# The causal mask in two attention layers: added by VectorE in a buffer instead of by products on TensorE

## The chip, the cores and the metric

The kernel runs as one program on one core of a Trainium2 chip. The metric is the device time of one execution in microseconds (us); the median of several runs is compared. Five engines work side by side, each in its own order, and wait for one another by semaphores: PE (TensorE, the matrix engine), DVE (VectorE), ACT (ScalarE), POOL (GpSimd) and SP (SyncE, which only issues DMAs here). PE writes its products into PSUM; DVE and ACT read them there.

## The reference, cut to what matters

The model is a tower of nine layers over 32 utterances of T = 93 frames and 256 channels: a tokenizer, then attention and feed-forward layers in turn. Four of the layers are attentions, and all four run through the same helper functions. The two that are changed are the first (called gated, names that begin with `gattn`) and the second (routed, `rattn`); both have 16 heads of width 16 and a causal mask. The first one, for example:

```python
scores = jnp.einsum('bhqd,bhkd->bhqk', q, k) * scale
causal = jnp.tril(jnp.ones((s, s), dtype=bool))
scores = jnp.where(causal[None, None], scores, -jnp.inf)
probs = jax.nn.softmax(scores / TEMP, axis=-1)
probs = probs * gate
out = jnp.einsum('bhqk,bhkd->bhqd', probs, v)
```

The third (differential, `dattn`) has 32 causal maps for each utterance, the fourth (`eattn`) has 16 heads and no mask.

## The kernel before, in words

**What a map goes through.** Each utterance has 16 score maps of 93x93. Four maps make a unit (93x372 numbers, one PSUM bank); an utterance has four units, `w` = 0 to 3, in two pairs, `p` = 0 and 1. The scores are computed twice. The first time, with queries on the partitions (tile `scores`), they serve only to find the maximum of each row: DVE reduces each unit to `negmax`. The second time, turned (tile `scoresT`), the negated maxima are added by products with `maxT`, and ACT takes the exponential into `probs`. PE then weighs the values (`outputs`), DVE divides by the sums (`rden`, `ctx`), PE turns the result (`turn_ctx`, L581) and projects it (L593), and DVE adds it to `hidden`.

**Where the mask stands.** In a causal attention the mask of -1e30 has to be in the first scores before the maximum is taken. `scores(b, buf, p)` does it on PE: for each of the two units of a pair one product of the identity with `mask_q`, 372 columns in bf16 (L524), opens the bank, and the eight score products of the pair (L530) are added on top. In the turned scores the mask comes with `maxT` and is not touched by the change.

**The order on PE** is written out by hand in `utterance` of `attention_pe`. While utterance b is weighed, the first scores of b+1 are made: scores of pair 0 of b+1, turned scores of pair 0 of b, scores of pair 1 of b+1, `turn_ctx` of b-1, turned scores of pair 1, weighing of units 0 and 1, projection of b-1, weighing of units 2 and 3, `turn_max` (L540). Two utterances make one turn of a hardware loop. PE takes its instructions strictly in this order.

**The order on DVE** (`attention_dve`): the maxima of pair 0 (L663, twice), the division of b-1 (`context`: a reciprocal, L908, and a product, L909), the maxima of pair 1, the split of the maxima into two bf16 numbers (L671, L673), the addition of the output (L919, L921), the copy of `maxT` (L680) and a statistic of the new rows (L303).

**The waits around the change.** `scores` waits for the semaphore `maxed`, which each reduction raises, so the bank of the unit two before is free. `turn_ctx` waits for `ctx_ready`, which DVE raises after `context`. `cut` on POOL prepares the queries of the next utterance (L489) as soon as the turned scores of a pair are done.

Of the kernel before, what the change touches and what calls it, by code (L numbers as in the profile page):

```python
# [24 lines left out]
ALU = mybir.AluOpType  # L25
AX = mybir.AxisListType

P = 128
# [3 lines left out]
T = 93  # L32
# [4 lines left out]
GT = GU * T  # L37
# [314 lines left out]
class Attention:  # L352
# [11 lines left out]
    def __init__(self, s, maps, causal, exp_scale):  # L364
# [9 lines left out]
        self.k = s.sb("k", [P, 2, DC, T])  # L374
        self.only = s.sb("only", [P, self.variants])
        self.parts = maps // HEADS
        self.sel = s.sb("sel", [P, HEADS, T], BF16)
        self.negmax = s.sb("negmax", [P, maps])

# [5 lines left out]
        self.ctxT = s.sb("ctxT", [P, DC, T])  # L385
        if causal:
            self.mask_q = s.sb("mask_q", [P, 4, T], BF16)
        self.ps_s = s.ps("scores", [P, 2, 512])
        self.ps_t = s.ps("scoresT", [P, 2, 512])
        self.ps_o = s.ps("outputs", [P, 2, 512])  # L390
# [10 lines left out]
        self.cut_ready = s.sem("cut_ready")  # L401
        self.scored = s.sem("scored")
        self.maxed = s.sem("maxed")
        self.split_ready = s.sem("split_ready")
        self.max_turned = s.sem("max_turned")
        self.maxT_ready = s.sem("maxT_ready")
# [57 lines left out]
def attention_constants_dve(dve, a, ident):  # L464

    rows = ident[:, :].rearrange("p (h v e) -> p v h e", h=2, v=a.variants)
    dve.tensor_reduce(a.only[:, :], rows, AX.XY, ALU.add).then_inc(a.step, 1)
    dve.sem_inc(a.maxed, 2)
    dve.sem_inc(a.probs_ready, 2)
    dve.sem_inc(a.weighed, 4)  # L470
    dve.sem_inc(a.scoredT, 2 * a.units)
    dve.sem_inc(a.outputs_read, 3 - a.banks_o)
# [42 lines left out]
def attention_pe(pe, a, ident, ident16, w_out, before_out=None, extra_out=None):  # L515


    def scores(b, buf, p):
        if 2 * p % (a.units // DC) == 0:
            pe.wait_ge(a.cut_ready, DC * b + (2 * p * DC // a.units + 1))  # L520
        pe.wait_ge(a.maxed, b * a.units + (2 * p + 2))
        if a.causal:
            for half in range(2):
                pe.matmul(a.ps_s[0:T, half, 0:GT], ident16[:, 0:T], a.mask_q[:, :, :], start=True, stop=False,  # L524
                          skip_group_check=True)
        for j in range(4):
            for half in range(2):
                c, _, v = a.place(2 * p + half)
                rows = slice(half * P // 2, (half + 1) * P // 2)
                mm = pe.matmul(a.ps_s[0:T, half, j * T:(j + 1) * T], a.q[rows, buf, c, v + j, :], a.k[rows, buf, c, :],  # L530
                               start=not a.causal, stop=True, skip_group_check=True)
                if j == 3:
                    mm.then_inc(a.scored, 1)

# [83 lines left out]
    for p in range(a.units // 2):  # L618
        scores(0, 0, p)
# [36 lines left out]
def attention_dve(dve, a, steps, contexts, add, finish=None, shared=None):  # L656
# [1 line left out]

    def maximum(b, w):
        dve.wait_ge(a.scored, b * a.units + (w + 1))
        dve.tensor_reduce(a.negmax[0:T, a.first_map(w):a.first_map(w) + 4],  # L663
                          a.ps_s[0:T, w % 2, 0:GT].rearrange("p (j t) -> p j t", j=4), AX.X, ALU.max,
                          negate=True).then_inc(a.maxed, 1)

    def split(b):
        dve.wait_ge(a.maxed, 2 + (b + 1) * a.units)
# [26 lines left out]
    def utterance(b, buf, first, last):  # L695
        for p in range(a.units // 2):
            if not last:
                maximum(b + 1, 2 * p)
                maximum(b + 1, 2 * p + 1)
            if not first:  # L700
                behind(b - 1, 1 - buf, p)
        if not last:
            split(b + 1)
        if not first:
            add(b - 1)
        if not last:
            max_t(b + 1)
        if not first and shared is not None:
            measure_dve(dve, shared, b - 1, a.added, b)

    for w in range(a.units):
        maximum(0, w)
    split(0)
    max_t(0)
    over_utterances(dve, utterance)
# [2032 lines left out]
```

## Time and profile before

| what | us |
|---|---|
| median of 3 runs | 4184.95 |
| lowest and highest run | 4178.12, 4190.71 |
| the profiled execution, its own time | 4172.62 |
| its span, first to last instruction | 4170.9 |
| PE busy (79% of the span) | 3284.4 |
| DVE busy (50%) | 2086.2 |

A row of the trace names a line of the kernel (L524), an engine, an operation and the tiles out<-in. Matrix instructions overlap in their pipeline, so the distance from one start to the next tells more than their durations. The clock that TensorE was granted is shown as a share of full speed: 1.00 is 2.4 GHz and 0.50 is 1.2 GHz.

### The profile page before, as it was taken

How to read it: one execution, taken by the hardware profiler on the slowest of the kernel's cores; microseconds unless marked ns; L12 is line 12 of the kernel's file. 1: busy time of each engine (PE TensorE's matmuls, PEld its weight loads, DVE VectorE, ACT ScalarE, POOL GpSimd, SP SyncE). 2: the span in 40 equal slices, each digit the busy share in tenths (PEclk: the TensorE clock that was granted, in tenths of full speed). 3: DMA queues.
4: the chain of work that ended last, by engine and by line, in shares of the span. 5: the costliest groups of instructions: out<-in, count | busy, mean ns of one | idle time of the engine just before them, and what ended most of it. 6: DMA issues, size and time to landing. Idle time of an engine off the chain costs nothing. (4 is left out here: it accounts for less than half of the span.)

```text
span 4170.9 us, 70241 instructions
## 1 busy us (share of the span) xinstructions
PE 3284.4 (79%) x23447; PEld 2210.8 (53%) x23448; DVE 2086.2 (50%) x4029; ACT 1232.1 (30%) x2459; POOL 1221.4 (29%) x934
## 2 busy tenths in 40 slices
PE   7589981649997699999606996478888887579999
PEld 3357761326775367777505995234334333256777
DVE  0444437323445245555542333478888888731443
ACT  2222110011121122222213442265555565413222
POOL 0102110102120124334171002656556555510221
PEclk9698875778888899999658998689888888769998
DMA  1000000570000200000241112222212221100000
GB/s 46 12 1 0 0 2 11 88 97 1 0 0 11 88 1 0 0 0 0 70 137 50 45 50 60 74 58 54 52 46 58 52 52 52 36 10 0 9 11 10
DMA packets 250482, 140.02 MB, mean 34 GB/s; under 512 B 175329, under 2 KB 226467, under 8 KB 250384
## 3 DMA queue, kind: packets, MB, share of 16 engines
q1 hardware_dynamic: 230480, 122.61, 12.0%
q0 software_dynamic: 18432, 12.40, 1.3%
q10 hardware_dynamic: 1472, 3.85, 0.3%
q8 instruction: 43, 0.70, 0.1%
q14 instruction: 55, 0.45, 0.0%
HBM read 103.41 MB, written 35.21 MB: 33 GB/s over the span
## 5 line engine op out<-in xcount | busy, mean ns | idle before, releaser
L2414 DVE TENSOR_TENSOR_SCAN ssm_state<-ssm_dA,ssm_dBx 128x372 f32<-128x372 f32 x512 | 434.3, 910 | 103.3 <-ACT ssm_dA L2203 82.6
L2109 POOL TENSOR_TENSOR ssm_dBx<-ssm_du,ssm_bc_wide 128x1488 f32<-128x1488 f32 x128 | 426.9, 3340 | 196.5 <-DVE ssm_state L2414 195.1
L2288 PE MATMUL ssm_y<-ssm_hC,top_ident 128*128 128x512 f32 (+1 forms) x768 | 405.9, 671 | 93.8 <-DVE ssm_hC L2419 86.6
L2203 ACT ACTIVATE ssm_dA<-ssm_delta,ssm_decay 128x368 f32<-128x368 f32 x512 | 276.7, 565 | 190.9 <-DVE ssm_state L2414 179.2
L2288 PEld LDWEIGHTS ssm_y<-ssm_hC,top_ident 128*128 128x128 f32 x768 | 157.6, 216 | 307.9 <-issue 165.2
L2419 DVE TENSOR_TENSOR ssm_hC<-ssm_state,ssm_c_wide 128x1488 f32<-128x1488 f32 x128 | 218.1, 1704 | 5.1
L643 ACT ACTIVATE dattn_probs<-dattn_scoresT 93x372 f32<-93x372 f32 x256 | 108.1, 472 | 350.9 <-PE dattn_scoresT L556 350.9
L570 PE MATMUL dattn_outputs<-dattn_v,dattn_probs 93*93 (+1 forms) x2048 | 185.4, 233 | 0.0
L570 PEld LDWEIGHTS dattn_outputs<-dattn_v,dattn_probs 93*93 93x93 f32 x2048 | 181.8, 163 | 3.4
L489 POOL TENSOR_TENSOR rattn_q<-rattn_q_all,rattn_only 128x372 f32<-128x372 f32 x64 | 51.7, 807 | 439.6 <-PE rattn_scoresT L556 247.2
L1409 POOL TENSOR_TENSOR dattn_square<-dattn_square,top_minus_half 93x16 f32<-93x16 f32 x32 | 92.7, 2896 | 271.9 <-DVEq L1485 271.9
L489 POOL TENSOR_TENSOR eattn_q<-eattn_q_all,eattn_only 128x372 f32<-128x372 f32 x64 | 51.6, 807 | 403.3 <-PE eattn_scoresT L556 217.0
L663 DVE TENSOR_REDUCE dattn_negmax<-dattn_scores 93x4 f32<-93x372 f32 x256 | 127.1, 536 | 82.5 <-PE dattn_scores L530 79.7
L2251 PE MATMUL ssm_misc<-ssm_xT,ssm_w_tap 128*128 128x364 f32 (+3 forms) x512 | 165.9, 477 | 2.6 <-ACT ssm_conv L2140 2.0
L489 POOL TENSOR_TENSOR gattn_q<-gattn_q_all,gattn_only 128x372 f32<-128x372 f32 x64 | 51.7, 807 | 334.0 <-PE gattn_scoresT L556 248.8
L489 POOL TENSOR_TENSOR dattn_q<-dattn_q_all,dattn_only 128x744 f32<-128x744 f32 x64 | 91.6, 1432 | 170.6 <-ACT dattn_k_all L781 98.0
L1535 PE MATMUL tiles_hidden<-tiles_x_part,moe_w 128*128 128x256 bf16 x496 | 136.4, 275 | 3.0 <-DVE tiles_x_part L1889 3.0
L1901 DVE TENSOR_TENSOR tiles_act<-tiles_gelu,tiles_act 128x512 bf16<-128x512 f32 x124 | 85.8, 692 | 102.4 <-ACT tiles_act L1827 102.4
L1537 PE MATMUL tiles_hidden<-tiles_x_part,moe_w 128*128 128x256 bf16 x496 | 136.4, 275 | 0.0
L1536 PE MATMUL tiles_hidden<-tiles_x_part,moe_w 128*128 128x256 bf16 x496 | 136.4, 275 | 0.0
L2251 PEld LDWEIGHTS ssm_misc<-ssm_xT,ssm_w_tap 128*128 128x128 f32 x512 | 98.1, 192 | 70.5 <-issue 13.7
L1535 PE MATMUL tiles_product<-moe_w,tiles_act 128*128 x496 | 135.2, 273 | 0.0
(546 smaller groups left out, 7209.1 us busy)
## 6 DMA issues: line engine op xcount, KB each, us to landing
ssm_bc_wide<-bc_rows SPq DMA_DIRECT2D x128, 372.0 KB, 4.3
route_stage<-in_L_ffn_W SPq DMA_DIRECT2D x32, 512.0 KB, 4.2
qkv_rows<-rattn_rows SPq DMA_DIRECT2D x32, 288.0 KB, 3.1
rattn_heads<-qkv_rows SPq DMA_DIRECT2D x96, 96.0 KB, 3.5
moe_sent<-top_blank SPq DMA_DIRECT2D x1, 7936.0 KB, 23.6
tiles_x_in<-moe_sent SPq DMA_DIRECT2D x31, 256.0 KB, 2.8
moe_back<-tiles_y SPq DMA_DIRECT2D x31, 256.0 KB, 2.1
tok_frames<-in_frames ACTq DMA_DIRECT2D x8, 376.0 KB, 8.4
```

What stands on the lines that cost most here:

```text
L489: pool.tensor_tensor(a.q[:, buf, c, :, :], a.q_all[:, c, bass.ds(b * T, T)].unsqueeze(1).broadcast_to([P, a.variants, T]), a.only[:, :].un ...
L570: mm = pe.matmul(a.ps_o[0:T, bank, h * (HD + 1):(h + 1) * (HD + 1)], a.probs[0:T, w % 4, j * T:(j + 1) * T], a.v[0:T, b, h, :], start=True ...
L663: dve.tensor_reduce(a.negmax[0:T, a.first_map(w):a.first_map(w) + 4], a.ps_s[0:T, w % 2, 0:GT].rearrange("p (j t) -> p j t", j=4), AX.X, A ...
L1535: pe.matmul(out, w_high, x_high, start=start, stop=False)
L1536: pe.matmul(out, w_high, x_low, start=False, stop=False)
L1537: return pe.matmul(out, w_low, x_high, start=False, stop=stop)
L2109: pool.tensor_tensor(dBx[:, k % 2, :, :], du[:, :, :], bc_wide[:, q % BUFS, 0, k % 2, :].unsqueeze(1).broadcast_to([P, CC, GT]), ALU.mult) ...
L2203: act.activation(by_utterance(dA[:, ring(k, c), 0:GT])[:, :, 1:], by_utterance(delta[:, c, :])[:, :, 1:], ACT.Exp, scale=decay[:, c, k:k + ...
L2251: mm = pe.matmul(by_utterance(ps_m[:, 0:GT])[:, :, back:], w_tap[:, TAPS - 1 - back, c, m * P:(m + 1) * P], by_utterance(n.xT[:, c, :])[:, ...
L2288: mm = pe.matmul(ps_y[:, at], ident[:, :], hC[:, k % 2, :, :].rearrange("p c t -> p (c t)")[:, at], start=(k == 0), stop=(k == N - 1), ski ...
L2414: dve.tensor_tensor_scan(state[:, k % 2, c, :], dA[:, ring(k, c), 0:GT], dBx[:, k % 2, c, :], 0.0, ALU.mult, ALU.add).then_inc(scanned, 1)
L2419: dve.tensor_tensor(hC[:, k % 2, :, :], state[:, k % 2, :, :], ps_c[:, 0:GT].unsqueeze(1).broadcast_to([P, CC, GT]), ALU.mult).then_inc(hc ...
```

## The change

In attentions that are causal and have 16 maps (`masked_early`: gated and routed), `scores` loses its two mask products a pair, and the score products open their bank themselves. DVE adds `mask_q` to the scores of each unit and writes the sum as f32 into a new buffer `masked` in SBUF, and reduces the maxima from there. PE's wait for a free bank is on the new semaphore `scores_masked`, raised by the addition, in place of `maxed`. The differential attention keeps its products and the expert attention has no mask, but for these too the two reductions of a pair now stand behind both waits for the two units' scores.

```diff
@@ Attention.__init__
+        self.masked_early = causal and self.parts == 1
+            self.masked = s.sb("masked", [P, 2, 4, T]) if self.parts == 1 else None
+        self.scores_masked = s.sem("scores_masked")
@@ attention_constants_dve
+    dve.sem_inc(a.scores_masked, 2)
@@ attention_pe, scores
-        pe.wait_ge(a.maxed, b * a.units + (2 * p + 2))
-        if a.causal:
+        pe.wait_ge(a.scores_masked if a.masked_early else a.maxed, b * a.units + (2 * p + 2))
+        if a.causal and not a.masked_early:
             for half in range(2):
                 pe.matmul(a.ps_s[0:T, half, 0:GT], ident16[:, 0:T], a.mask_q[:, :, :], start=True, stop=False,
                           skip_group_check=True)
...
-                               start=not a.causal, stop=True, skip_group_check=True)
+                               start=not a.causal or a.masked_early, stop=True, skip_group_check=True)
@@ attention_dve
-    def maximum(b, w):
-        dve.wait_ge(a.scored, b * a.units + (w + 1))
-        dve.tensor_reduce(a.negmax[0:T, a.first_map(w):a.first_map(w) + 4],
-                          a.ps_s[0:T, w % 2, 0:GT].rearrange("p (j t) -> p j t", j=4), AX.X, ALU.max,
-                          negate=True).then_inc(a.maxed, 1)
+    def maxima(b, p):
+        for w in (2 * p, 2 * p + 1):
+            dve.wait_ge(a.scored, b * a.units + (w + 1))
+            if a.masked_early:
+                dve.wait_ge(a.maxed, b * a.units + (w + 1))
+                dve.tensor_tensor(a.masked[0:T, w % 2, :, :], a.ps_s[0:T, w % 2, 0:GT].rearrange("p (j t) -> p j t", j=4),
+                                  a.mask_q[0:T, :, :], ALU.add).then_inc(a.scores_masked, 1)
+        for w in (2 * p, 2 * p + 1):
+            if a.masked_early:
+                dve.wait_ge(a.scores_masked, b * a.units + (w + 3))
+                found = a.masked[0:T, w % 2, :, :]
+            else:
+                found = a.ps_s[0:T, w % 2, 0:GT].rearrange("p (j t) -> p j t", j=4)
+            dve.tensor_reduce(a.negmax[0:T, a.first_map(w):a.first_map(w) + 4], found, AX.X, ALU.max,
+                              negate=True).then_inc(a.maxed, 1)
```

How the instructions stand on PE at the head of the gated attention's loop, before (ISA and REGISTER_ALU are waits and counts of the sequencer; x8 means eight in a row):

```order
L521 ISA
L524 MATMUL gattn_scores<-gattn_mask_q,top_ident 93x372 x2
L530 MATMUL gattn_scores<-gattn_k,gattn_q 93x93 x8
L545 ISA
L549 MATMUL gattn_scoresT<-gattn_q,gattn_k 93x372 x2
L556 MATMUL gattn_scoresT<-gattn_maxT,gattn_sel 93x93 x8
L520 REGISTER_ALU
L521 REGISTER_ALU
L524 MATMUL gattn_scores<-gattn_mask_q,top_ident 93x372 x2
L530 MATMUL gattn_scores<-gattn_k,gattn_q 93x93 x8
L581 MATMUL gattn_general<-top_ident,gattn_ctx 128x93 x2
```

And now, at the same place:

```order
L525 ISA
L534 MATMUL gattn_scores<-gattn_k,gattn_q 93x93 x8
L549 ISA
L553 MATMUL gattn_scoresT<-gattn_q,gattn_k 93x372 x2
L560 MATMUL gattn_scoresT<-gattn_maxT,gattn_sel 93x93 x8
L524 REGISTER_ALU
L525 REGISTER_ALU
L534 MATMUL gattn_scores<-gattn_k,gattn_q 93x93 x8
L585 MATMUL gattn_general<-top_ident,gattn_ctx 128x93 x2
```

The two mask products ahead of each set of score products are gone; nothing else on PE has moved.

On DVE, in the second utterance of the same loop, before:

```order
L662 REGISTER_ALU
L663 TENSOR_REDUCE gattn_negmax<-gattn_scores 93x4 x2
L908 RECIPROCAL gattn_rden<-gattn_outputs 93x16
L736 ISA
L909 TENSOR_TENSOR gattn_ctx<-gattn_outputs,gattn_rden 93x256
```

And now:

```order
L667 REGISTER_ALU
L670 TENSOR_TENSOR gattn_masked<-gattn_scores,gattn_mask_q 93x372 x2
L674 REGISTER_ALU
L678 TENSOR_REDUCE gattn_negmax<-gattn_masked 93x4
L674 REGISTER_ALU
L678 TENSOR_REDUCE gattn_negmax<-gattn_masked 93x4
L921 RECIPROCAL gattn_rden<-gattn_outputs 93x16
L749 ISA
L922 TENSOR_TENSOR gattn_ctx<-gattn_outputs,gattn_rden 93x256
```

Two additions of 93x372 stand ahead of the two reductions, and the reciprocal and the product of `ctx`, for which `turn_ctx` on PE waits, come behind four operations in place of two.

## Rows read from the trace of the kernel before

**Rows 1.** Busy time by stretch: gated, routed, expert attention; `PEclk` is the clock.

```profile
276.00:602.00 326.00, 317.03 (x3127) 228.16 (x3126) 135.24 (x376) 63.40 (x158) 60.71 (x120) 0.87 0.00 0
942.00:1270.00 328.00, 318.85 (x3118) 228.81 (x3118) 135.22 (x376) 63.19 (x157) 63.58 (x126) 0.86 0.00 0
3858.00:4150.00 292.00, 282.64 (x3168) 221.87 (x3170) 124.46 (x347) 69.88 (x187) 60.72 (x120) 0.99 0.03 10
```

**Rows 2.** Instructions by tile: count, ns min/median/max, first and last start.

```profile
L524 PE MATMUL gattn_scores<-gattn_mask_q,top_ident x128: 321/358/543, 275.7 to 590.3; 128*93 128x372 bf16 x128
L663 DVE TENSOR_REDUCE gattn_negmax<-gattn_scores x128: 530/536/543, 278.1 to 591.9; 93x4 f32<-93x372 f32 x128
...
L524 PE MATMUL rattn_scores<-rattn_mask_q,top_ident x128: 321/358/543, 942.2 to 1259.3; 128*93 128x372 bf16 x128
```

**Rows 3.** Timeline of PE at full clock: start, length, line, tiles, count.

```profile
404.05 0.51 PE L524 MATMUL gattn_scores<-gattn_mask_q,top_ident 128*93 128x372 bf16 x2
404.49 0.90 PE L530 MATMUL gattn_scores<-gattn_k,gattn_q 64*93 64x93 f32 x16
...
406.47 0.52 PE L524 MATMUL gattn_scores<-gattn_mask_q,top_ident 128*93 128x372 bf16 x2
...
407.74 0.38 PE L581 MATMUL gattn_general<-top_ident,gattn_ctx 93*128 93x93 f32 x2
```

**Rows 4.** Timeline of DVE in the same utterance.

```profile
405.42 0.99 DVE L663 TENSOR_REDUCE gattn_negmax<-gattn_scores 93x4 f32<-93x372 f32 x2 [0.68 <-PE gattn_scores L530]
406.33 0.24 DVE L908 RECIPROCAL gattn_rden<-gattn_outputs 93x16 f32<-93x16 f32 x1
406.61 0.42 DVE L909 TENSOR_TENSOR gattn_ctx<-gattn_outputs,gattn_rden 93x256 f32<-93x256 f32 x1
```

**Rows 5.** Timeline of PE in the expert attention, which has no mask.

```profile
3898.57 0.90 PE L530 MATMUL eattn_scores<-eattn_k,eattn_q 64*93 64x93 f32 x16
...
3901.38 0.38 PE L581 MATMUL eattn_general<-top_ident,eattn_ctx 93*128 93x93 f32 x2
```

**Rows 6.** DVE additions of a PSUM and an SBUF tile, by tile.

```profile
L919 DVE TENSOR_TENSOR gattn_summed<-gattn_general,gattn_o_bias x32: 420/421/421, 301.1 to 612.6; 93x256 f32<-93x256 f32 x32
...
L1331 DVE TENSOR_TENSOR rattn_rows<-rattn_outputs,rattn_bias x16: 670/687/689, 746.1 to 907.5; 93x512 f32<-93x512 f32 x16
```

**Rows 7.** Timeline of PE: the `turn_max` that closes five utterances in a row.

```profile
403.83 0.20 PE L540 MATMUL gattn_general<-top_ident,gattn_split 93*32 93x93 bf16 x1
...
412.87 0.20 PE L540 MATMUL gattn_general<-top_ident,gattn_split 93*32 93x93 bf16 x1
...
422.30 0.23 PE L540 MATMUL gattn_general<-top_ident,gattn_split 93*32 93x93 bf16 x1
...
432.68 0.23 PE L540 MATMUL gattn_general<-top_ident,gattn_split 93*32 93x93 bf16 x1
...
444.72 0.20 PE L540 MATMUL gattn_general<-top_ident,gattn_split 93*32 93x93 bf16 x1
```

**Rows 8.** Busy time by stretch, the same columns as Rows 1, two stretches of 6.83 us.

```profile
425.75:432.58 6.83, 6.83 (x78) 5.41 (x76) 2.90 (x9) 2.02 (x5) 2.02 (x4) 1.00 0.00 0
432.58:439.41 6.83, 6.46 (x49) 4.06 (x50) 2.15 (x6) 0.84 (x2) 1.01 (x2) 0.50 0.00 0
```

**Rows 9.** Timeline of PE in the utterance at half clock.

```profile
433.28 0.85 PE L524 MATMUL gattn_scores<-gattn_mask_q,top_ident 128*93 128x372 bf16 x2 [0.37 <-issue]
434.06 1.57 PE L530 MATMUL gattn_scores<-gattn_k,gattn_q 64*93 64x93 f32 x16
...
437.47 0.83 PE L524 MATMUL gattn_scores<-gattn_mask_q,top_ident 128*93 128x372 bf16 x2
...
439.60 0.38 PE L581 MATMUL gattn_general<-top_ident,gattn_ctx 93*128 93x93 f32 x2
```

**Rows 10.** POOL's product in Rows 4's utterance; a DVE product of the differential attention.

```profile
406.68 0.81 POOL L489 TENSOR_TENSOR gattn_q<-gattn_q_all,gattn_only 128x372 f32<-128x372 f32 x1 [5.13 <-PE gattn_scoresT L556]
...
L1491 DVE TENSOR_TENSOR dattn_ctx<-dattn_diff,dattn_square x32: 421/1644/1652, 1517.5 to 2021.8; 93x256 f32<-93x256 f32 x32
```

More of the change, by code:

```diff
@@ L697, in utterance @@
             if not last:
-                maximum(b + 1, 2 * p)
-                maximum(b + 1, 2 * p + 1)
+                maxima(b + 1, p)
             if not first:
@@ L709, in utterance @@
             measure_dve(dve, shared, b - 1, a.added, b)
-    for w in range(a.units):
-        maximum(0, w)
+    for p in range(a.units // 2):
+        maxima(0, p)
     split(0)
```

## The prediction

> **What bounds the kernel now.** I read the busy time by stretch first: it tells which engine is full in the two stages that the change touches. In the gated attention PE is busy 317 of 326 us and in the routed one 319 of 328, while DVE is busy 135 us in each [rows 1]. So PE sets the pace there, and DVE has room on average. The same rows hold a second thing: the granted clock is 0.87 and 0.86 in these two stages, but 0.99 in the expert attention, which runs the same loop without mask products and with a few others, on a PE that is about as busy (283 of 292 us). Next I read the tile view, for what the change takes away: 128 mask products in each stage (32 utterances, four units) [rows 2]. Then I read the timelines of one utterance, since a share of busy time does not tell whether DVE is free at the moment when PE needs it. Last come the distances between utterances and the clock in between [rows 7, 8].
>
> **What is removed.** At full clock a pair's two mask products take 404.49 - 404.05 = 0.44 us until the score products start [rows 3], so 0.88 us an utterance. At half clock they take 434.06 - 433.28 = 0.78 us [rows 9]. If PE were never kept waiting, 31 utterances at 0.88 us in two stages would give 55 us. That is not what I expect, because of where DVE stands.
>
> **What is added on DVE, and who waits for it.** No row shows the new addition. It has an f32 operand in PSUM and one in SBUF, as two forms do that are in the trace: 421 ns at 256 columns and 687 ns at 512 [rows 6]; at 372 that gives 421 + 116/256 x 266 = 541 ns, as an estimate between these two rows. That mask_q is bf16 could make it less; I take no gain from that. The reduction takes 536 ns from PSUM [rows 2]; from SBUF I take the same. Two reductions in a row take 0.99 us together [rows 4], so the second starts 0.45 us behind the first, and the reciprocal behind them starts 406.33 - 405.42 = 0.91 us after the first: 0.455 us an operation.
>
> Now PE's wait. `turn_ctx` (L581) needs `ctx`, and `ctx` stands on DVE behind the maxima of pair 0. Before, counted from the start of the pair's score products: the first reduction starts at 405.42 - 404.49 = 0.93 us [rows 3, 4], `ctx` is done at 407.03 - 404.49 = 2.54, and PE comes to `turn_ctx` at 407.74 - 404.49 = 3.25, 0.7 us later. DVE had that much room. Counted from the start of the utterance (with the mask products, 0.44 us earlier) `turn_ctx` stands at 3.69 us.
>
> After, the utterance starts with the score products. First addition at 0.93 us, four operations at 0.455 us, so reciprocal at 2.75, the product of `ctx` 0.28 us later [rows 4] at 3.03, done at 3.45. PE follows a DVE result by some 0.06 us (the maxima end at 406.41, the next mask product starts at 406.47) [rows 3, 4]. So `turn_ctx` can start at 3.51 us, against 3.69 before. PE alone would be there earlier: in the expert attention, without mask products, it is there 3901.38 - 3898.57 = 2.81 us after the start [rows 5]. At full clock, then, PE waits 0.7 us for DVE in each utterance, and the utterance gains 0.18 us and not 0.88. The rest of the utterance is as before: behind `ctx` DVE still has the maxima of pair 1, the split and the addition of the output, and the second additions end about 1 us after `ctx`, at 4.5 us, far ahead of the next utterance.
>
> The new waits cost something too: the loop on DVE has four more waits a pair, and each reduction of `masked` waits for DVE's own addition. The addition of unit 0 is long done when its reduction comes, since unit 1's stands between them. I take 0.1 us an utterance where DVE is late, between 0 and 0.34 (below).
>
> **The utterances at half clock.** The starts of `turn_max` are 9.04, 9.43, 10.38 and 12.04 us apart, 40.89 us for four utterances [rows 7]; this round repeats through most of the loop. The first two run at full clock; the other two have stretches at 0.50 of the clock in their first half, of which rows 8 show the longer one. In the longest utterance `turn_ctx` stands at 439.60 - 433.28 = 6.32 us [rows 9]. Without its two sets of mask products, 0.78 and 0.76 us (the score products follow at 438.23), it is at 4.78. DVE's chain starts later here: the score products end at 435.63, 1.57 us after their start, DVE follows 0.03 us later, as at full clock (404.49 + 0.90 to 405.42) [rows 3, 4], and with the 2.58 us from first addition to `turn_ctx` that makes 4.18 us from the utterance's start. PE is later than DVE, so nothing waits. I do not book the whole 1.54 us as gained: if the stretch at half clock keeps its length, what comes next falls into its rest. What is taken away is then worth what it costs at full clock, 0.88 us. For the third utterance, whose stretch is shorter, the two are about level, and I take the same.
>
> **The sum.** Four utterances gain 2 x (0.18 - 0.1) + 2 x 0.88 = 1.92 us. A stage has 31 utterances that make scores for the next one, 7.75 rounds of four, so 14.9 us; two stages 29.8 us. The first scores of each stage, before the loop, lose two sets of mask products and get two pairs of additions; I leave this out, it is under 1 us. The differential and the expert attention wait for both units before the first reduction; the two halves of a pair run abreast on PE, so the second is done one product after the first, at most 0.05 us (0.73 us for 16). With up to five pairs an utterance that is between 0 and 8 us; I take 0, since the second reduction had to wait for the second unit before as well. A gain of 30 us on the profiled execution, 4172.6 us, gives 4142.6. The median of the runs is 12.3 us above that execution; I take the gain from the median: **4155 us**.
>
> **Rivals.** (a) *DVE's operations do not overlap.* Then four take 4 x 0.54 = 2.16 us and not 1.82; `turn_ctx` comes at 3.85, and the full-clock utterance loses 0.16 us. Four utterances gain 2 x (-0.16 - 0.1) + 1.76 = 1.24 us, both stages 19 us: 4166. For it: each reduction now has a wait of its own. Against it: the 0.99 us for two of 536 ns [rows 2, 4]. The Trainium skill states such a rule (page "VectorE: DVE Perf Modes", section "The DRAIN you can't avoid"): the next operation does not start until the pipe is empty. By that rule the time would be this rival's; the trace shows an overlap of 0.08 us.
>
> (b) *The clock gets worse.* In rows 8 PE is busy 6.83 of 6.83 us, and the clock falls all the same; what is done ahead of the fall is weighing and projection, which the change leaves as it is, but the loop falls into another step with it, and PE now stands still 0.7 us an utterance. A further utterance of the 10.38 kind in four costs 10.38 - 9.04 = 1.34 us, which leaves 0.58 us, 9 us in all: 4176. One of the 12.04 kind costs 12.04 - 9.43 = 2.61 and leaves -0.69 us, so 11 us slower: 4196. The Trainium skill (page "TensorE: Matmul & The Clock Gate", section "What's actually happening") says that half rate is the default and that activity releases it, which speaks for this rival; no row here shows what a wait of 0.7 us does.
>
> (c) *The clock gets better.* If the loop ran at full clock throughout, as the expert attention nearly does [rows 1], four utterances would take 2 x (9.04 + 9.43 - 0.16) = 36.6 us and not 40.9: 4.3 us, 66 us in all: 4119. Against it: the expert attention has additional products beside its projection, which these two lack.
>
> (d) *Slower: POOL holds up DVE's reads.* A product of DVE whose operands both lie in SBUF takes 1644 ns in the differential attention in the median, 421 at best [rows 10]; the long ones run while POOL works. In the gated attention POOL's product starts 406.68 - 404.49 = 2.19 us after the score products and lasts 0.81 us [rows 10], right across the new reductions from SBUF. If such a reduction were held up by the same 1.22 us, `turn_ctx` would come at 3.51 + 0.1 + 1.22 = 4.83 at full clock (1.14 us later than before) and at 5.50 at half clock, of whose 0.88 us 0.16 would be left: -1.96 us for four, 30 us slower: 4215. It decides from a hold of 0.7 us on. Against it: the reduction has a single operand, and the product of `ctx`, from PSUM and SBUF, takes 0.42 us with POOL's product running beside it [rows 4, 10].
>
> That the products stay is excluded by the order of instructions.
>
> **Chances.** The forecast 0.60 (its own range 4142 to 4165: at the low end no 0.1 us of new waits, and the products at half clock worth 1.21 us, halfway to 1.54, which makes 2.78 us for four and 43 in all; at the high end nearly (a)), (a) 0.15, (b) 0.11, (c) 0.07, (d) 0.07. A measurement of this kernel can tell about 0.3%, 12.5 us, from no change. Faster by more: 0.58 of the forecast, 0.11 of (a), 0.07 of (c), 0.02 of (b), so 0.78. Slower by more: (d) 0.07 and the worse end of (b) 0.03, so 0.10. Within it: 0.12. The range reaches from (c), 4119, to just above (b)'s milder case, 4180; it leaves out (d), the rest of (b) and the half of (c) beyond its time, about 0.15.
>
> **What would show it.** Right: `turn_ctx` in the gated attention has an idle time ahead of it that DVE's `ctx` ends, about 0.7 us at full clock and none at half clock; at full clock `turn_max` comes about 8.9 and 9.3 us apart; four DVE operations from the first addition to the reciprocal take about 1.8 us; the mask rows are gone; the clock of the two stages stays near 0.87. Rival (a) shows as 2.2 us for these four, (b) and (c) as a clock below 0.8 or above 0.95 in the two stages, (d) as reductions over 1 us. The prediction is wrong in its main step if PE does not wait for `ctx`: then the gain is nearer to 55 us.

## The result, and the profile after

The changed kernel takes **4209.15 us** (median; 4191.73 to 4210.89), against 4184.95 before. The ratio is 1.0046, 95% interval 1.0033 to 1.0059: some 19 us slower, where I had forecast 30 us faster. The changed kernel's runs lie in two groups, 4192 to 4196 and 4209 to 4211 us, and the median falls into the upper one; the two medians are 24 us apart, and the ratio, which weighs all runs, gives 19. The profiled execution of the changed kernel took 4191.73 us; a second profile of each kernel is drawn on below.

Busy time by stretch for the changed kernel, the same columns and stretches as [rows 1] (gated, routed, expert attention; the figure behind the five engines is the granted clock):

```profile
276.00:602.00 326.00, 302.91 (x2995) 232.15 (x2993) 206.42 (x515) 63.38 (x158) 62.82 (x125) 0.83 0.00 0
942.00:1270.00 328.00, 295.40 (x2981) 227.60 (x2982) 202.49 (x502) 65.47 (x161) 64.67 (x128) 0.83 0.03 3
3858.00:4150.00 292.00, 280.42 (x2986) 216.10 (x2985) 116.80 (x324) 69.49 (x187) 62.61 (x124) 0.98 0.03 9
```

PE has lost 14 and 23 us of work, DVE has gained some 70 us in each stage, and the clock has fallen from 0.87 and 0.86 to 0.83. (In the routed stretch part of the 23 us is that the loop begins 15 us later, at 965 and not at 950.) The stretches hold all but the same work as before, in the same time: what PE no longer does, it waits or does more slowly.

The timeline of one utterance of the changed kernel at full clock, PE first (start, length, line, tiles, count; in brackets the idle time ahead and what ended it), answers to [rows 3]:

```profile
422.51 0.20 PE L544 MATMUL gattn_general<-top_ident,gattn_split 93*32 93x93 bf16 x1
422.73 0.90 PE L534 MATMUL gattn_scores<-gattn_k,gattn_q 64*93 64x93 f32 x16
...
426.27 0.38 PE L585 MATMUL gattn_general<-top_ident,gattn_ctx 93*128 93x93 f32 x2 [0.67 <-DVEq L925]
...
431.39 0.20 PE L544 MATMUL gattn_general<-top_ident,gattn_split 93*32 93x93 bf16 x1
...
440.66 0.20 PE L544 MATMUL gattn_general<-top_ident,gattn_split 93*32 93x93 bf16 x1
```

And DVE's in the same utterance, which answers to [rows 4]:

```profile
423.65 0.99 DVE L670 TENSOR_TENSOR gattn_masked<-gattn_scores,gattn_mask_q 93x372 f32<-93x372 f32 x2 [0.23 <-PE gattn_scores L534]
424.56 0.97 DVE L678 TENSOR_REDUCE gattn_negmax<-gattn_masked 93x4 f32<-93x372 f32 x2
425.46 0.24 DVE L921 RECIPROCAL gattn_rden<-gattn_outputs 93x16 f32<-93x16 f32 x1
425.74 0.42 DVE L922 TENSOR_TENSOR gattn_ctx<-gattn_outputs,gattn_rden 93x256 f32<-93x256 f32 x1
```

This is the utterance that was forecast. The reciprocal comes 425.46 - 423.65 = 1.81 us after the first addition (I had 1.82), `turn_ctx` 426.27 - 422.73 = 3.54 us after the start (3.51), behind a wait of 0.67 us (0.7); the next two `turn_max` are 8.88 and 9.27 us away (8.9 and 9.3), against 9.04 and 9.43 before [rows 7]. The addition takes 536 ns (541), the reduction from SBUF 526 ns, by tile (ns min/median/max):

```profile
L670 DVE TENSOR_TENSOR gattn_masked<-gattn_scores,gattn_mask_q x128: 530/536/543, 281.0 to 594.3; 93x372 f32<-93x372 f32 x128
L678 DVE TENSOR_REDUCE gattn_negmax<-gattn_masked x128: 525/526/528, 282.0 to 595.2; 93x4 f32<-93x372 f32 x128
```

So the mechanism at full clock holds, and the kernel is slower all the same. The experiments ask where the rest went. A table tells it, in us, each pair of numbers from two profiles of the same kernel. The way from one loop to the next goes from the last `turn_max` of the gated attention to the first of the routed one.

| part | before | after | change of the means |
|---|---|---|---|
| gated loop | 313.4, 313.2 | 312.8, 309.9 | -2 |
| way to the routed loop | 353.1, 353.8 | 366.3, 367.6 | +13.5 |
| routed loop | 315.9, 315.2 | 306.2, 312.3 | -6 |
| differential loop | 512.9, 518.7 | 529.8, 529.7 | +14 |
| expert loop | 284.6, 284.6 | 290.3, 290.5 | +6 |

Three of the five get worse, in stages of which the prediction expected nothing. All that is left of the kernel took 2391 and 2403 us before, and 2385 and 2400 after. In what follows, the time of a loop at half clock is the part of it for which the trace has a granted clock of 0.50; the mean clock tells the same (0.88 over 313 us means that 24% of it, 75 us, were at 0.50).

### The profile page after: what moved, and what is told of

It reads as the page before. It is cut to its first block and busy times, and to the rows that moved or that the text cites. A ratio compares the mean times of both kernels' runs of the same rounds, so it can differ in the third digit from the quotient of the medians.

```text
span 4189.9 us, 70403 instructions
## 1 busy us (share of the span) xinstructions
PE 3253.9 (78%) x23191; PEld 2211.9 (53%) x23192; DVE 2226.6 (53%) x4285; ACT 1232.4 (29%) x2459; POOL 1221.5 (29%) x934
## 5 line engine op out<-in xcount | busy, mean ns | idle before, releaser
L2301 PEld LDWEIGHTS ssm_y<-ssm_hC,top_ident 128*128 128x128 f32 x768 | 157.9, 216 | 312.8 <-issue 163.6
```

The source lines that it names most:

```text
L2301: mm = pe.matmul(ps_y[:, at], ident[:, :], hC[:, k % 2, :, :].rearrange("p c t -> p (c t)")[:, at], start=(k == 0), stop=(k == N - 1), ski ...
```

## The experiments

In the expectations, theory A is the new order of waits in the differential and the expert attention, theory B the clock in the gated and the routed loop, and theory C that this clock falls because of what PE does around the projection. Ratios are to the runs of the kernel before that were made beside each.

**Both kernels once more.** For these no code is changed.

> The kernel before, profiled once more. Theory that what differs between the two first profiles outside the four attention loops is the chance of an execution: the way from the gated loop's end to the routed loop's start is 353 or about 368 us long, and need not be the 353 of the first profile; the differential loop may have more time at half clock than 24 us. Rival, both belong to the code: 353 us and 513 us again.

> The changed kernel, profiled once more. Theory (chance of an execution): 353 or 368 us from the gated to the routed loop, gated and routed loops with half-clock time of 75 to 110 us each, expert loop 290.3 us again, utterances of 8.88, 9.15 us again. Rival (belongs to the code): 366 us again.

Measured: the second values of the table, 4190.18 and 4211.32 us. The way between the loops belongs to the code. The differential loop varies in the kernel before; in the changed one it was 529.8 and 529.7 us.

**The way to the routed loop: a buffer's address.** The routed layer writes its rows to DRAM and reads them back into `rattn_heads`, in pieces of 16 f32 numbers, 64 bytes. The new buffer `masked` takes 2976 bytes a partition and stands ahead of `rattn_heads`, which moves from byte 181568 to 184544: from a multiple of 64 to one of 32 only.

```diff
 e13 (to before, behind mask_q):
+            self.unused = s.sb("unused", [P, 2, 4, T]) if self.parts == 1 else None
 e17 (the same, 2944 bytes):
+            self.unused = s.sb("unused", [P, 736]) if self.parts == 1 else None
 e14 (to after, behind masked):
+            self.pad = s.sb("pad", [P, 24]) if self.parts == 1 else None
```

> The kernel before with one thing added: a buffer of 2976 bytes a partition that nothing reads or writes, where the change has masked. It moves the buffer rattn_heads from address 181568 to 184544, a multiple of 32 bytes and no more of 64. Theory: that is why the routed layer's transfers from qkv_rows into rattn_heads (pieces of 64 bytes) land in 4.8 us and not in 3.5, and the way from the gated to the routed loop is 367 us long and not 353: 4185 + 14 = 4199 us. Rival, what costs there is the mask's new code or chance: 353 us and 4185 us.

> The changed kernel with an unused buffer of 96 bytes a partition behind masked, so that rattn_heads lies on a multiple of 64 bytes again (184640). Theory: 353 us from the gated to the routed loop, 4209 - 14 = 4195 us. Rival: 367 us and 4209 us.

> The kernel before with an unused buffer of 2944 bytes a partition in place of e13's 2976: rattn_heads moves nearly as far, to 184512, which is a multiple of 64 bytes. Theory (only the place against 64 bytes counts): 353 us from the gated to the routed loop, transfers landing in 3.5 us. Rival (any move of the buffer does it): 367 us and 4.8 us.

Measured: e13 4203.09 us (ratio 1.0029, 1.0013 to 1.0046), e14 4190.76 us (1.0016, 1.0000 to 1.0032), against 1.0046 for the change as it is. The page's list of DMA issues (count, KB each, median us from issue to landing) has in the changed kernel:

```profile
rattn_heads<-qkv_rows SPq DMA_DIRECT2D x96, 96.0 KB, 4.8
```

in e13, which is the kernel before with an unused buffer:

```profile
rattn_heads<-qkv_rows SPq DMA_DIRECT2D x96, 96.0 KB, 4.9
```

and in e14, the changed kernel with 96 unused bytes:

```profile
rattn_heads<-qkv_rows SPq DMA_DIRECT2D x96, 96.0 KB, 3.5
```

which is what the kernel before has, too, and e17 (one run, 4191.69 us). The whole way to the routed loop, busy time by stretch with the DMA share next to last, in e13 and then in e14:

```profile
597.00:967.90 370.90, 162.36 (x681) 95.98 (x681) 143.91 (x287) 29.63 (x62) 24.29 (x24) 0.64 0.45 56
```

```profile
597.40:949.20 351.80, 154.63 (x678) 91.54 (x677) 146.43 (x291) 29.61 (x62) 24.27 (x24) 0.66 0.40 59
```

The same bytes keep the DMA engines busy for 0.45 x 370.9 = 167 us in e13 and for 0.40 x 351.8 = 141 us in e14. The buffer's place alone does it. By the ratios it costs 1.0046 - 1.0016 = 0.30%, 12.5 us. e17's transfers land in 3.5 us, as expected for 64 bytes, but its way took 361.3 us:

```profile
595.10:956.40 361.30, 161.60 (x682) 95.90 (x681) 143.54 (x287) 29.61 (x62) 24.43 (x24) 0.65 0.39 57
```

The DMA engines were busy 0.39 x 361.3 = 141 us, as with e14's multiple of 64, so the moved buffer didn't make the transfers dearer; where the other 8 us come from stays open. The Trainium skill (page "DMA: Bandwidth & Descriptors", section "How a descriptor splits into AXI transactions") says of reads that each transaction has to start at a multiple of 256 bytes, so that a transfer which starts elsewhere begins with one from the multiple below. By it, if it held for the written side too, one of four pieces at 32 beyond a multiple of 64 would take two transactions, since it crosses a multiple of 256, and none at a multiple of 64. The 3.5 and 4.8 us agree in direction, but the packets of the trace don't show one in four: of the 147456 packets of 64 bytes in e13, 2.7% took over 14 ns, against 0.01% in the kernel before, and the others mostly the same 11 ns in both. No run here tells that boundary from others.

**The order of waits in the two attentions that keep their way of masking.** Before, each reduction stands behind its own wait. In the change both waits stand ahead of the first reduction.

```diff
 e1 and e15 (to after), in the two attentions that are not masked early, in short:
-        for w in (2 * p, 2 * p + 1):
-            dve.wait_ge(a.scored, b * a.units + (w + 1))
         for w in (2 * p, 2 * p + 1):
+            dve.wait_ge(a.scored, b * a.units + (w + 1))
             dve.tensor_reduce(a.negmax[0:T, a.first_map(w):a.first_map(w) + 4], found, AX.X, ALU.max,
 e3 (to after):
-            dve.wait_ge(a.scored, b * a.units + (w + 1))
+            if w % 2 == 0:
+                dve.wait_ge(a.scored, b * a.units + (2 * p + 2))
```

e15 has the 96 bytes of e14 as well. e2 is the kernel before with both waits ahead of the two reductions in all four attentions, and nothing else.

> The changed kernel, but in the differential and the expert attention each reduction stands right behind its own wait again, as before the change. Theory A (the loss comes from the two waits that now stand ahead of the first reduction in the two attentions that were not meant to change): the loop of the expert attention goes back from 290.4 to 284.6 us between the first and the last turn_max, that of the differential one from 529.7 to 512.9 us, and the time falls by some 23 us, to about 4186. Theory B (the loss comes from the clock in the gated and the routed attention, which have 103 and 86 us at half clock where there were 74 and 80): nothing changes, about 4209.

> The kernel before, with the mask products, and only the order of waits from the change: in all four attentions both waits for the scores of a pair stand ahead of the first of its two reductions. Theory A: the differential and the expert attention cost what they cost in the changed kernel, 17 and 6 us more than before, and the gated and the routed one some 0.1 us an utterance where PE starts its second mask products right behind the maxima, 0 to 6 us together: about 4210. Theory B: as the kernel before, 4185.

> The changed kernel with one wait a pair, for the second unit's scores, in place of one for each unit. The first reduction thus still waits for both units, but the sequencer has no second count to work out between the first wait and the reduction. Theory A1 (the time goes into working out the second wait's count once the first wait is over): the expert attention goes back to 9.03 and 9.42 us an utterance, the differential one to 16.27, and the time to about 4186 as in e1. Theory A2 (the time goes into waiting for the second unit's scores): as the changed kernel, 9.15 and 9.51, 16.5, about 4209.

> The same 96 bytes and the old order of waits in the differential and the expert attention: the change without its two side effects. Theory: e1_old_waits' 4187 - 14 = 4173 us, 0.3% faster than before. What is then left against the 4155 us of the prediction is the time at half clock in the gated and the routed loop.

Measured: e1 4187.33 us (0.9994, 0.9976 to 1.0012), e2 4197.94 us (1.0042, 1.0027 to 1.0057), e3 4152.06 us (0.9927, 0.9902 to 0.9952), e15 **4170.01 us** (0.9967, 0.9953 to 0.9981). In the expert attention of the changed kernel, the scores of both pairs on PE and the first reductions on DVE:

```profile
3938.97 0.90 PE L534 MATMUL eattn_scores<-eattn_k,eattn_q 64*93 64x93 f32 x16
...
3941.06 0.90 PE L534 MATMUL eattn_scores<-eattn_k,eattn_q 64*93 64x93 f32 x16
```

```profile
3940.01 0.99 DVE L678 TENSOR_REDUCE eattn_negmax<-eattn_scores 93x4 f32<-93x372 f32 x2 [0.71 <-PE eattn_scores L534]
```

And the same in e15:

```profile
3912.07 0.90 PE L535 MATMUL eattn_scores<-eattn_k,eattn_q 64*93 64x93 f32 x16
...
3914.05 0.90 PE L535 MATMUL eattn_scores<-eattn_k,eattn_q 64*93 64x93 f32 x16
```

```profile
3913.00 0.99 DVE L681 TENSOR_REDUCE eattn_negmax<-eattn_scores 93x4 f32<-93x372 f32 x2 [0.60 <-PE eattn_scores L535]
```

The first reduction comes 1.04 us after the first score product, and 0.93 with the old order. Over all pairs at full clock the median is 1.02 us with two waits (after and e2), 0.97 with one wait for the second unit (e3), 0.93 with the old order. So 0.04 us is the wait for the second unit, and 0.05 the second wait itself, with the working out of its count. PE's scores of the second pair wait for these maxima and come 3941.06 - 3938.97 = 2.09 us after the first, not 1.98. So an utterance of the expert attention takes 9.15 us instead of 9.03, and the next 9.51 instead of 9.42. That is 3 us in the loop, and it is what e2's loop has more (287.7 us); in the changed kernel it is 6 us more, with 9.7 us at half clock instead of 3.4. In the differential attention an utterance takes 16.46 us instead of 16.27. That makes 6 us there; its loop is 529.7 to 529.8 us with two waits (after twice, e2, e14) and 512.9 to 525.5, 519.3 in the mean, in the twelve profiles with the old order and the same work. So the 14 us of the table, against two profiles, are rather 10. The rest is the clock, in busy time by stretch over the loop of the changed kernel's second profile, and of the second one of before:

```profile
1502.40:2032.00 529.60, 524.08 (x5946) 388.91 (x5946) 291.55 (x700) 117.17 (x278) 189.81 (x150) 0.95 0.00 0
```

```profile
1494.30:2013.00 518.70, 516.47 (x5947) 384.26 (x5948) 290.37 (x700) 117.17 (x278) 189.83 (x150) 0.96 0.00 0
```

In the changed kernel the loop spends 58 us at half clock both times, in the kernel before 24 and 38, and up to 55 with the old order elsewhere. By the ratios of e14 and e15 the order of waits costs 1.0016 - 0.9967 = 0.49%, 20.5 us; e2 has it alone, in all four attentions, at 0.42%, less than was expected. e15, the change without its two side effects, is 0.33% faster than before. e3 was a surprise: its expert utterance took 9.08 us, halfway as its wait has it, but most of its gain came from the gated and routed loops, which took 298.5 and 293.2 us, although its full-clock utterances there are longer than those of the change (9.02 us). They spent 54 and 42 us at half clock, not 103 and 86. By stretch:

```profile
280.40:578.90 298.50, 276.82 (x2940) 212.43 (x2940) 199.79 (x490) 62.15 (x154) 60.71 (x120) 0.91 0.00 0
945.20:1238.40 293.20, 271.08 (x2940) 207.08 (x2940) 198.43 (x490) 62.13 (x154) 60.70 (x120) 0.93 0.00 0
```

That leads to the clock.

**The clock in the gated and the routed loop.** First, what are the mask products worth if DVE adds nothing? e8 leaves the mask out of the routed attention's first scores (the mask in the turned scores stays); e7 adds on DVE, and PE keeps its products, whose sums are overwritten.

```diff
 e8 (to e1):
-        self.masked_early = causal and self.parts == 1
+        self.masked_early = False
+        self.unmasked = causal and self.parts == 1 and exp_scale < 1.0
-        if a.causal and not a.masked_early:
+        if a.causal and not a.unmasked:
-                               start=not a.causal or a.masked_early, stop=True, skip_group_check=True)
+                               start=not a.causal or a.unmasked, stop=True, skip_group_check=True)
 e7 (to e1):
-        if a.causal and not a.masked_early:
+        if a.causal:
-                pe.matmul(a.ps_s[0:T, half, 0:GT], ident16[:, 0:T], a.mask_q[:, :, :], start=True, stop=False,
+                pe.matmul(a.ps_s[0:T, half, 0:GT], ident16[:, 0:T], a.mask_q[:, :, :], start=True, stop=a.masked_early,
```

> The kernel before, with the mask left out of the first scores of the routed attention (so its maxima are those of all scores; the turned scores are masked as before) and nothing in its place: the products' removal alone, in one stage. If PE alone sets the pace there without them, full-clock utterances of 8.2 and 8.6 us in the routed attention, 0.85 us less than before: 26 us less in the loop at the same share of half clock, about 4158. If something else ends late: less than 10 us.

> As e1, but PE does the mask products all the same, and the score products then overwrite them: the additions alone, without what they save. If turn_ctx waits for ctx 3.51 us after the first score product, that is 3.95 us after the start of the utterance where it was 3.69: full-clock utterances 0.2 to 0.3 us longer than before, 9.3 and 9.7, and about 4185 + 16 = 4200 before the clock has its say. If DVE's additions were hidden: 9.04 and 9.47 as before, 4185.

Measured: e8 4188.84 us (1.0011, 0.9993 to 1.0028), e7 4213.90 us (1.0072, 1.0047 to 1.0096). Both carry the address's 12 us (their way to the routed loop is 369.0 and 372.4 us), which the expectations didn't know; so do e1, e3, e4, e5, e9 and e10, and not e6. e7's full-clock utterance is 9.33 us, as forecast for a `turn_ctx` that waits for DVE's chain. The routed loop of e8, by stretch:

```profile
964.20:1269.20 305.00, 299.29 (x2939) 230.41 (x2939) 131.76 (x366) 62.18 (x154) 60.85 (x120) 0.82 0.00 0
```

At full clock its utterances take 8.15 us instead of 9.04, which is the whole 0.88 us of the prediction. 31 x 0.88 = 27 us should go; 315.5 - 305.0 = 10.5 went. The loop's time at half clock rose from 80 to 112 us. So even for free the products are worth less than half of their time: without them PE spends more of the loop at half clock.

Next, is it the wait of 0.67 us? e4 puts the reciprocal and the product of `ctx` between the additions and the reductions, so that `turn_ctx` need not wait. And is it the work ahead of the projection, of which the expert attention has more? e5 adds two products there that nothing reads, as large as two of the expert attention's.

```diff
 e4 (to e1), attention_dve:
-            if not last:
-                maxima(b + 1, p)
+            if not last and a.masked_early:
+                additions(p, b + 1)
+            if not last and not a.masked_early:
+                reductions(p, b + 1)
             if not first:
                 behind(b - 1, 1 - buf, p)
+            if not last and a.masked_early:
+                reductions(p, b + 1)
 e5 (to e4), e6 (to before), e9 (to e1), in the gated and the routed attention:
+                def filler(b):
+                    for c in range(DC):
+                        pe.matmul(a.ps_g[:, 1, 0:T], w_out[:, c, 0:P], a.ctxT[:, c, :], start=(c == 0), stop=(c == DC - 1))
-                attention_pe(pe, a, ident, ident16, w_out)
+                attention_pe(pe, a, ident, ident16, w_out, filler)
```

e10 is e5 with these products in the differential attention too, and e16 is e10 with the 96 bytes of e14.

> As e1, and in the gated and the routed attention the reciprocal and the product of ctx stand between the additions and the reductions of pair 0, so that turn_ctx on PE waits for two DVE operations fewer. If PE's wait for ctx is what keeps the removed products from being a gain at full clock: full-clock utterances of 8.2 and 8.6 us in place of 8.89 and 9.27, 0.7 us for each of 62 utterances, about 43 us less than e1: 4143. If the clock takes it back: more time at half clock in the two stages, and not under 4175.

> As e4, with two products more an utterance in the gated and the routed attention, ahead of the projection, at the place and in the size of those of the expert attention (L2614 there); what they compute is never read. Theory C (the clock falls because of what PE does around the projection, and such products keep it up, as in the expert attention, whose loop has 3.4 us at half clock): 0.5 us more an utterance at full clock, 8.64 and 9.03 us, so some 274 us a loop, with under 15 us at half clock; e4 had 287 and 298 us with 72 and 98 at half clock. That makes about 4117, with more work. Against theory C: half-clock time as in e4, and 0.5 us for each of 62 utterances on top: 4186.

> The kernel before, mask products and all, with the same two unread products more an utterance in the gated and the routed attention. Theory C: full-clock utterances of 9.54 and 9.93 us, a loop of some 302 us with little half-clock time in place of 313 and 316 with 74 and 80: about 4160, faster with more work. Against it: 31 us slower, 4216.

> The changed kernel, with the old order of waits in the differential and the expert attention, and with the two unread products an utterance ahead of the projection in the gated and the routed attention. Theory: with the clock held up, only the step at full clock is left of the change, and it is as large as the prediction had it (turn_ctx waits for DVE's chain): an utterance of 9.49 - 0.17 = 9.32 us, against 9.49 in the kernel before with the same products; 62 utterances x 0.17 = 10.5 us less than that kernel's 4151, so 4141 us. Rival, PE alone sets the pace: 8.61 us an utterance, 4097 us. Rival, the clock falls as in the changed kernel: 4187 us or more.

Measured, with the time of the two loops and what of it was at half clock (us):

| kernel | median, ratio (95%) | full-clock utterance | gated loop, at half | routed loop, at half |
|---|---|---|---|---|
| before | 4184.95 | 9.04 | 313.4, 74 | 315.9, 80 |
| e1, old waits | 4187.33, 0.9994 (0.9976 to 1.0012) | 8.88 | 308.0, 90 | 305.5, 84 |
| e4, ctx first | 4155.13, 0.9939 (0.9917 to 0.9960) | 8.14 | 287.1, 72 | 298.3, 98 |
| e9, e1 filled | 4195.65, 1.0032 (1.0018 to 1.0047) | 9.33 | 315.3, 65 | 309.0, 46 |
| e6, before filled | 4151.36, 0.9924 (0.9900 to 0.9949) | 9.49 | 300.6, 6 | 299.1, 4 |
| e5, e4 filled | **4116.01**, 0.9836 (0.9813 to 0.9860) | 8.59 | 274.3, 10 | 273.7, 9 |

In e4 PE comes from the scores to `turn_ctx` without a wait:

```profile
396.79 0.90 PE L534 MATMUL gattn_scores<-gattn_k,gattn_q 64*93 64x93 f32 x16
397.62 0.38 PE L585 MATMUL gattn_general<-top_ident,gattn_ctx 93*128 93x93 f32 x2
```

Its two loops are 28 us shorter than e1's, not 43: in e1 PE waits the 0.67 us in 36 of the 62 utterances, and where the clock is at half it doesn't wait. 36 x (8.88 - 8.14) = 27 us.

The gated loop by stretch in e6, e9 and e5, in this order:

```profile
283.70:584.20 300.50, 294.12 (x3183) 220.10 (x3183) 131.73 (x366) 62.12 (x154) 60.72 (x120) 0.99 0.00 0
```

```profile
282.60:597.90 315.30, 294.47 (x3060) 231.62 (x3060) 198.76 (x490) 62.18 (x154) 60.85 (x120) 0.90 0.00 0
```

```profile
283.30:557.60 274.30, 268.31 (x3060) 211.54 (x3060) 187.76 (x490) 62.14 (x154) 60.71 (x120) 0.98 0.00 0
```

e6 does more than the kernel before, 0.45 us an utterance, and is 0.8% faster, because the clock stays at 0.99. I had expected the same of e9, 4141 us, and was wrong: e9 has the same products, and its clock is 0.90 (of the 55 us by which it missed, 12 are the address). What it has and e5 has not is the wait ahead of `turn_ctx`, in e9's timeline of PE:

```profile
404.81 0.90 PE L534 MATMUL gattn_scores<-gattn_k,gattn_q 64*93 64x93 f32 x16
406.38 0.38 PE L585 MATMUL gattn_general<-top_ident,gattn_ctx 93*128 93x93 f32 x2 [0.67 <-DVEq L936]
...
409.19 0.66 PE L878 MATMUL gattn_general<-gattn_ctxT,gattn_w_out 128*128 128x93 f32 x4
```

and in e5's:

```profile
410.64 0.90 PE L534 MATMUL gattn_scores<-gattn_k,gattn_q 64*93 64x93 f32 x16
411.47 0.38 PE L585 MATMUL gattn_general<-top_ident,gattn_ctx 93*128 93x93 f32 x2
...
414.27 0.66 PE L882 MATMUL gattn_general<-gattn_ctxT,gattn_w_out 128*128 128x93 f32 x4
```

So beside the added products the wait of 0.67 us costs twice: 0.74 us an utterance at full clock (9.33 - 8.59), and the clock, 65 and 46 us at half instead of 10 and 9. Without the added products taking the wait away doesn't hold the clock up: e4 has none, and 72 and 98 us at half clock. The Trainium skill (page "TensorE: Matmul & The Clock Gate", section "What's actually happening") says that activity releases the clock. e6 and e9 agree in direction; e3 and e8 don't speak for it, with PE busy 277 of 298.5 us at 0.91 and 299 of 305 us at 0.82 (in part because the same products keep PE busy longer at half clock). What makes the clock fall is not shown: why e3, with a wait and without added products, has 54 and 42 us at half clock and the change 103 and 86 stays open.

**Both kernels beaten.**

> The run with ctx ahead of the reductions and the unread products, 4116 us, with the same two unread products in the differential attention too. Theory that the products hold the clock up wherever they stand ahead of the projection: the differential loop, 522.6 us with 48 us at half clock, has 31 utterances of 16.26 + 0.45 us = 518 us and hardly a stretch at half clock: 4111 us. Rival, they only add work there: 14 us more, 4130 us.

> e10_all_filled with the same 96 bytes: 4110 - 14 = 4096 us by the theory, 4110 by the rival.

Measured: e10 4110.39 us (0.9825, 0.9794 to 0.9857). Its differential loop took 519.2 us with 7 us at half clock; without the products there, e5 took 522.6 us with 48. So the time at half clock went, as the theory had it, and the rival's 14 us more are excluded; but 3 us are less than lie between the two profiles of the kernel before (512.9 and 518.7), and a gain in time there is not shown. e16 took **4090.31 us** (0.9773, 0.9749 to 0.9798), 2.3% less than before, with all that the runs taught: `ctx` first, the clock held up, the address mended, the old order of waits.

## Why the prediction was wrong

The prediction was 4155 us, a gain of 30; the kernel lost 19. By the ratios the 49 us between are 12.5 of the address, 20.5 of the order of waits, and 16 by which the change itself fell short (e15's -0.33% is 14 us). By the intervals of the ratios each of the three is good to some 6 to 9 us.

- **The chain on DVE**: right, to 0.03 us; PE waits for it in 35 of the 62 utterances, where half had been booked, and in none at half clock, as forecast. DVE's operations overlap as in [rows 4]; rivals (a) and (d) fall with it. Of 128 reductions from SBUF in the gated attention none took more than 528 ns, so POOL's product doesn't hold them up.
- **The new waits in the gated and the routed attention**, booked at 0.1 us an utterance: too much. The full-clock utterance gained 9.04 - 8.88 = 0.16 us, not 0.08, so they cost 0.02.
- **The utterances at half clock**: wrong. The step that failed is that a stretch at half clock keeps its length, and the next falls into its rest. By it these utterances were to bring 2 x 0.88 us in four, 27 of the 30 us. In the changed kernel the two loops spent 103 and 86 us at half clock, and 95 and 101 the second time, not 74 and 80. In the first profile of the changed kernel there is a kind of utterance that the kernel before doesn't have (its longest is 12.09 us), from one `turn_max` to the next in the timeline of PE,

```profile
331.10 0.24 PE L544 MATMUL gattn_general<-top_ident,gattn_split 93*32 93x93 bf16 x1
...
346.20 0.26 PE L544 MATMUL gattn_general<-top_ident,gattn_split 93*32 93x93 bf16 x1
```

15.10 us long and at half clock from end to end, as the busy time by stretch has it:

```profile
331.00:351.48 20.48, 20.11 (x143) 15.18 (x142) 9.14 (x24) 2.86 (x7) 3.05 (x6) 0.50 0.00 0
```

e15, which is free of the other two causes, shows what is left: 308.2 and 306.3 us for loops that took 313.4 and 315.9, 15 us of the 30. Rival (b) had the direction. Of its cause, PE's standstill, the runs show only a part: with the added products the wait brings the half-clock time back (e9 against e5), but without them taking it away helps nothing (e4 against e1: 170 and 174 us in the two loops), and taking products away brings more half-clock time with no wait at all (e8).
- **Both waits ahead of the first reduction**, booked at 0 with bounds of 0 and 8 us: the step that cost most, 20.5 us. I took it that the second reduction had to wait for its unit anyway, but it is the first one that is held up, by 0.09 us, and PE's next scores wait for its maxima. I had no price for a second wait at all. At full clock the two together cost 6 us in the differential and 3 in the expert loop, about the upper bound (which counted five pairs an utterance, where there are six); what they cost in clock, some 4 us in the differential loop and 3 in the expert one, comes on top.
- **The buffer**: no step of the prediction spoke of it. I costed the operations that write and read `masked`, and not that it moves all buffers behind it. The row that would have warned, the page's 3.5 us for transfers into `rattn_heads`, was there; what it depends on was not to be seen in one profile.
- The range, 4119 to 4180, reached up only to one mild case of (b). The two costs above lay in stages that I had dismissed in two sentences.

## What to carry to other kernels

Price a change in every stage that runs its helper, and look at where its new buffers push the others: here the stages that should not have changed cost 33 us, more than the change was to bring. Time taken from an engine whose clock moves can be worth less than its length (two fifths in e8), and a wait on it more (e9 against e5); look at the granted clock of the loop before and after, and not only at the longest wait. Where a dependent result and other work stand in one queue, put the result first: `ctx` ahead of the reductions was worth 0.74 us in every utterance that waited.

## What the runs showed of the hardware

- DMAs in pieces of 64 bytes into a buffer at a multiple of 32 bytes that is not one of 64 landed in 4.8 to 4.9 us, and in 3.5 us at a multiple of 64 (e13, e14, e17).
- Two products that nothing reads, 0.45 us an utterance, raised the granted clock of the loop from 0.88 to 0.99 and made the kernel before 0.8% faster (e6). With a wait of 0.67 us in the utterance they raised it only from 0.85 (e1) to 0.90 (e9).
- A second wait ahead of a DVE operation, with its count, cost about 0.05 us: the first reduction came 1.02 us after the scores' start with two waits, and 0.97 with one for the later unit.
